# Attention and mixture-of-experts block on one core: order of the last attention group, projection in two halves, gate logits laid out by row

## The reference

```python
x = x + xattn(layernorm(x), ctx_512, Wq, w_kc_q, w_kc_kv, W_qr, W_kr, Wo)
x = x + ffn(layernorm(x), gate_weight, bias, w1, w3, w2, ws1, ws3, ws2)

# in xattn
attn    = softmax(scores)                       # per head
ctx_c   = einsum('bhsl,bld->bhsd', attn, kv_r)  # the value products
ctx_lat = einsum('bhsd,hkd->bhsk', ctx_c, w_kc_kv)
return ctx @ Wo.T                               # the projection

# in ffn
logits = x @ gate_weight.T
scores = sigmoid(logits)                        # then the routing
topk_idx, tw = choose 2 of 4 groups, then 4 of 32 experts by scores + bias
return sum over chosen experts of tw * swiglu_e(x) + swiglu_shared(x)
```

## Time and profile before

| | |
|---|---|
| median of three runs | 302.06 us |
| profiled execution, its own time | 301.82 us |
| span of the profiled execution | 299.5 us |
| outside the span | 2.3 us |
| PE busy | 282.5 us, 94% of the span |
| DVE busy | 181.4 us, 61% |
| ACT busy | 156.4 us, 52% |
| share of PE in the chain that ended last | 85% |
| mean granted PE clock | 0.995 |

### The profile page before, as it was taken

One profiled execution on the slowest core, in us unless ns is written; L12 is line 12 of the kernel. 1 busy time (PEld: TensorE's weight loads), 2 busy tenths in 40 slices (PEclk: granted clock), 3 DMA queues, 4 the chain that ended last, 5 costly groups with the idle time before them and its releaser, 6 DMA issues.

```text
span 299.5 us, 5458 instructions
## 1 busy us (share of the span) xinstructions
PE 282.5 (94%) x1831; PEld 202.7 (68%) x1831; DVE 181.4 (61%) x434; ACT 156.4 (52%) x373; POOL 129.5 (43%) x121
## 2 busy tenths in 40 slices
PE   8988799999999999999999999978789999999982
PEld 6857568676777666787667777754567666676662
DVE  4877776576757777765854466158842233344676
ACT  2747469675785866777773355185212333343330
POOL 0656328791036770079940000000176555565572
PEclk9999999999999999999999999999999999999998
DMA  7962500001700001600039992402033544432234
GB/s 235 402 253 79 204 1 2 0 2 25 255 3 1 0 3 46 218 0 1 2 127 380 402 352 78 173 2 70 1 106 106 150 150 144 154 109 72 70 82 130
DMA packets 15994, 34.41 MB, mean 115 GB/s; under 512 B 2528, under 2 KB 8416, under 8 KB 15968
## 3 DMA queue, kind: packets, MB, share of 16 engines
q1 hardware_dynamic: 13664, 27.77, 26.0%
q0 software_dynamic: 2304, 6.29, 7.4%
HBM read 30.38 MB, written 3.67 MB: 114 GB/s over the span
## 4 chain that ended last, share of the span: by engine, by line
PE 85%; DVE 7%; DMA 2%; issue 2%; ACT 2%; POOL 1%; POOLq 0%; DVEq 0%; ACTq 0%
PE bank L719 10%; PE bank L612 10%; PE bank L595 9%; PE bank L583 5%; PE bank L562 5%; PE bank L584 4%; PE bank L740 4%; PE bank L456 4%; PE bank L458 4%; PE bank L457 4%; PE bank L505 3%; PE bank L708 3%; PE bank L537 3%; PE bank L685 3%; PE bank L540 3%; PE bank L463 2%
## 5 line engine op out<-in xcount | busy, mean ns | idle before, releaser
L1413 POOL DMA_INDIRECT rope<-xn_rows,idx x32 | 31.2, 974 | 83.3 <-DVE idx L1307 61.9
L893 ACT ACTIVATE prob<-bank,nmax 128x512 f32<-128x512 f32 x48 | 32.7, 685 | 38.9 <-DVE nmax L1097 38.9
L361 POOL TENSOR_TENSOR rtmp<-abuf,rope 128x512 f32<-128x512 f32 x20 | 25.7, 1284 | 60.4 <-PE bank L458 41.0
L1097 DVE TENSOR_REDUCE nmax<-bank 128x1 f32<-128x512 f32 x64 | 41.2, 685 | 8.7 <-PE bank L584 8.4
L719 PE MATMUL bank<-wall,nmat 128*64 (+1 forms) x256 | 31.2, 386 | 0.8 <-ACT nmat L968 0.8
L612 PE MATMUL bank<-pT,kvr 128*64 128x256 f32 x256 | 31.2, 386 | 0.0
L1115 DVE COPY pT<-bank 128x512 f32<-128x512 f32 x32 | 22.0, 687 | 13.1 <-PE bank L595 12.9
L583 PE MATMUL bank<-kdup,qsp 128*128 128x512 f32 x64 | 28.3, 442 | 1.2 <-ACT prob L893 1.2
L364 POOL TENSOR_TENSOR roped<-rtmp 128x512 f32<-128x512 f32 x20 | 25.9, 1295 | 1.6
L1314 DVE TENSOR_TENSOR kv<-bank,kv 128x256 f32<-128x256 f32 x16 | 6.8, 425 | 32.5 <-ACT kv L981 32.4
L595 PE MATMUL bank<-ident,prob 128*128 128x128 f32 x192 | 26.3, 273 | 0.0
(11 more groups left out here) (217 smaller groups left out, 559.8 us busy)
## 6 DMA issues: line engine op xcount, KB each, us to landing
wall<-in_w_exp SPq DMA_DIRECT2D x32, 384.0 KB, 7.5
wring<-in_w_attn SPq DMA_DIRECT2D x16, 224.0 KB, 4.3
wring<-in_w_attn SPq DMA_DIRECT2D x4, 640.0 KB, 8.1
y_rows<-nmat SPq DMA_DIRECT2D x10, 256.0 KB, 2.1
wring<-in_w_attn SPq DMA_DIRECT2D x4, 512.0 KB, 7.0
rope<-in_rope_q SPq DMA_DIRECT2D x1, 768.0 KB, 7.0
x_sb<-in_x SPq DMA_DIRECT2D x1, 512.0 KB, 3.6
xn_rows<-xn SPq DMA_DIRECT2D x4, 128.0 KB, 1.7
```

What stands on the lines that cost most here:

```text
L361: eng.tensor_tensor(t0.rearrange("p (b s) -> p b s", b=B), own.rearrange("p (b s) -> p b s", b=B), cos, ALU.mult)
L893: act.activation(probs[t % 4], s_ps[t % 3][:, :], ACT.Exp, bias=nmax[:, t:t + 1], accum_out=psum_e[:, t:t + 1]).then_inc(s_exp, 1)
L1097: dve.tensor_reduce(nmax[:, t:t + 1], s_ps[t % 3][:, :], AX.X, ALU.max, negate=True).then_inc(s_max, 1)
L1413: pool.indirect_dma_start(xg[:, u % XG, :], None, xn_dram, bass.IndirectOffsetOnAxis(idx[:, u:u + 1], 0)) \
```

## The change

Three things are changed. First, PE runs step `O 6` between `quotients(15)` and `attend(15)`; before, it came ahead of `attend(15)` with the quotients behind that. `attend(15)` now waits for ACT's copy of the quotients. Second, step `O 7` is cut in two: the half for batch 0 comes before the sums of the gate weights and waits for one `ctx` less, the half for batch 1 behind them. Third, the gate logits have the rows as PE's weights and stream the gate weights; they come out with the tokens on the partitions, in bank 6, and DVE's copy and PE's transpose fall away.

```diff
-            {0: "-P0 -P1 -P2", 2: "O0 O1 O2 O3", 8: "O4", 11: "S0", 15: "O5 O6"},
+            {0: "-P0 -P1 -P2", 2: "O0 O1 O2 O3", 8: "O4", 11: "S0", 15: "O5"},
...
             for n in range((TILES - 2 - ALAG) // 4 + 1, GRPS):
-                if n > (TILES - 1 - ALAG) // 4:
-                    attend(n)
+                pe.wait_ge(c_sum, n)
                 quotients(n)
-
+                step(NG, "O", NP - 2)
+                pe.wait_ge(c_half, n + 1)
+                attend(n)
+
+            def last_rows(k):
+
+                i = NP - 1
+                pe.wait_ge(wk_out, out_count(len(USED) - 1))
+                pe.wait_ge(c_sum, 2 * i + 1 + k)
+                for tt in range(2 * k, 2 * k + 2):
+                    mm = pe.matmul(o_ps[k][:, (tt % 2) * D:(tt % 2 + 1) * D], ctT[:, i, tt * P:(tt + 1) * P], nmat[:, i, :],
+                                   start=False, stop=(tt % 2 == 1), skip_group_check=True)
+                mm.then_inc(o_mm, 1)
+
+            last_rows(0)
             pe.wait_ge(d_gate, 48)
             pe.wait_ge(d_moe, 16)
             for dc in range(ND):
                 mm = pe.matmul(gsum_ps, ones_e[:, 0:1].to_broadcast([P, P]), gateT[:, dc, :], start=(dc == 0), stop=(dc == ND - 1))
             mm.then_inc(gs_mm, 1)
-            step(NG, "O", NP - 1)
+            last_rows(1)
...
-            def logits_T(k):
-
-                for dc in range(ND):
-                    for tt in range(2 * k, 2 * k + 2):
-                        mm = pe.matmul(lgT_ps[tt * E:(tt + 1) * E, :], gateT[:, dc, :], xraw_T[:, dc, tt * P:(tt + 1) * P],
+            def logits(k):
+
+                for tt in range(2 * k, 2 * k + 2):
+                    for dc in range(ND):
+                        mm = pe.matmul(g_ps[:, tt * E:(tt + 1) * E], xraw_T[:, dc, tt * P:(tt + 1) * P], gateT[:, dc, :],
                                        start=(dc == 0), stop=(dc == ND - 1))
-                mm.then_inc(lgT_mm, 1)
+                mm.then_inc(lg_mm, 1)
...
-                logits_T(k)
-            pe.wait_ge(lgT_ev, 1)
-            pe.transpose(g_ps, lgT, ident[:, :]).then_inc(lg_mm, 1)
+                logits(k)
             keep_busy(6)
...
-            dve.wait_ge(lgT_mm, TT // 2)
-            dve.tensor_copy(lgT, lgT_ps).then_inc(lgT_ev, 1)
-            dve.wait_ge(lg_mm, 1)
+            dve.wait_ge(lg_mm, TT // 2)
```

More of the change, by code:

```diff
@@ L160, in build @@
         o_ps = bank[0:2]
-        lgT_ps = bank[7][:, 0:P]
         g_ps = bank[6][:, 0:P]
@@ L211, in build @@
         xraw_T = pT[:, :, :, :].rearrange("p r c s -> p (r c s)")[:, 0:ND * T].rearrange("p (d t) -> p d t", d=ND)
-        lgT = masked[:, :, :].rearrange("p t e -> p (t e)")
         eq_v = prob[:, 0, :]
@@ L272, in build @@
         gs_mm = sem("gs_mm"); gate_c = sem("gate_c")
-        lgT_mm = sem("lgT_mm"); lgT_ev = sem("lgT_ev"); lg_mm = sem("lg_mm"); lg_sc = sem("lg_sc")
+        lg_mm = sem("lg_mm"); lg_sc = sem("lg_sc")
         sh1_mm = sem("sh1_mm"); sh3_mm = sem("sh3_mm"); sh_silu = sem("sh_silu"); sh_gated = sem("sh_gated")
@@ L561, in step @@
                     for tt in range(TT):
[L562 to L566, removed]
+                        pe.matmul(o_ps[tt // 2][:, (tt % 2) * D:(tt % 2 + 1) * D], ctT[:, i, tt * P:(tt + 1) * P],
+                                       nmat[:, i, :], start=(i == 0 and tt % 2 == 0), stop=False, skip_group_check=True)
                 elif kind == "S":
```

## The result

The changed kernel takes 301.00 us in the median of 17 runs (300.05 to 302.32), the kernel before 302.15 in 17 runs beside it (301.67 to 303.49). The ratio is 0.9957, 95% interval 0.9946 to 0.9968: 1.0 to 1.6 us faster. The forecast was 301.2, with a range of 300.8 to 301.75, and 0.83 us. The profiled execution took 300.88 us with a span of 298.6, where 301.0 and 298.7 were forecast.

What follows compares the result with a forecast made beforehand. PE was taken to bound the kernel (busy 94% of the span), with time to win where the chain leaves it before the sigmoid. 0.74 (projection) + 0.09 (logits) = 0.83 us off the median 302.06 gave 301.2, range 300.8 to 301.75.

Steps and rivals of the forecast that it cites:

- Where the chain leaves PE: Time comes from stretches where the chain leaves PE, with 0.71 us idle ahead of the last projection, and PE's own work.
- Quotients first: Quotients and O6 ahead of the last value products: DVE's product ends 0.53 us earlier, with no work added.
- Halves: Last projection in halves: ACT's copy of the second half at 196.50 in place of 197.24, 0.74 us earlier.
- Logits: Gate logits with rows as weights: 0.72 us of steps removed, 0.09 us added to the gain at the sigmoid.
- Both bounds named: PE's 16 weight loads 0.113 us apart and ACT's table load with its small instruction both put the sigmoid near 200.10.
- 0.16 + 0.42: In the logits, what the wider loads take back, in us, of the 0.72 us removed.
- the loads are the limit, not the rows: In the logits, the second half's rows are ready at 198.47 while PE loads the first half until 198.63.
- The gain passes to the end: All behind the sigmoid counts from it, so the gain at the sigmoid is the gain at the end.
- The size: Whole kernel: 0.74 + 0.09 = 0.83 us gained, put on the median of 302.06.
- Slower: Rival at the logits: loads overlap nothing, 0.22 us apart, sigmoid 0.77 us later, time 302.8; 5%.
- half of it is absorbed: Rival: quotients wait for DVE or gather transfers take longer, 0.3 to 0.5 us lost, gain 0.4, time 301.65; 13%.
- More than forecast: Rival at the logits: ACT's load does not bind and PE's loads run faster, 0.74 + 0.37 = 1.1 us, time 300.95; 12%.

Runs made afterwards that it cites:

- hq: The changed kernel with the old logits, so quotients ahead and projection in halves only: 301.36 us, ratio 0.9973 to the kernel before.
- after: The changed kernel with all three changes, first trace: median 301.00 us, ratio 0.9957 to the kernel before; the profiled execution took 300.88 us.
- l_only: The kernel before with only the logits laid out by row: 301.64 us, ratio 0.9984.
- l_twice: The changed kernel with each logits matmul made twice, 32 weight loads in place of 16: 302.88 us, ratio 1.0029 to the kernel before.
- hl: The changed kernel with the quotients behind the value products again, halves and logits by row kept: 300.96 us, ratio 0.9967 to the kernel before.
- g_late: The changed kernel with the gate sums behind the second projection half and DVE's centring between its statistics pairs: 300.69 us, ratio 0.9968 to the kernel before.

## Why the prediction was right

- **Where the chain leaves PE.** Right. The idle 0.71 us is gone. The starts forecast up to the copy of the second half lie within 0.08 us on the trace's own clock, most of them within 0.03; counted from the last scores they come up to 0.15 late, the copy itself 0.07.
- **Quotients first.** The times were nearly right (DVE at 194.16, forecast 194.14, or 0.10 late counted from the last scores), the account was not. I wrote that 0.53 us of the gain "comes from the product being early". The halves alone give 0.78 us with the product as late as before; the early quotients on top of them cost 0.10 with the old logits and give 0.23 with the new ones. What they buy is the first copy of the rows free of the table load.
- **Halves.** 0.74 forecast; counted from the last scores the second copy moved by 0.67, so the term was 0.07 too large. Most of that arises by the start of the value products, 0.06 late, behind the wait ahead of the quotients. Two errors behind it cancel: the first half held PE for 0.97, not 0.88, and the gate sums for 0.36, not 0.45.
- **Logits.** 0.09 forecast on top, 0.14 found (hq to after). Both bounds named were there: loads 0.111 apart, and ACT's table load. In l_only 0.72 us of steps gone gave 0.15, because the 16 loads take longer than the old matmuls, and because ACT, whose small instruction started at 200.67 in the kernel before, could not have begun the sigmoid ahead of 200.78 with the same 0.11 behind it. The sum had 0.31 for the last matmul, where its own row said 0.28, and its line "0.16 + 0.42" leaves 0.14, not the 0.09 that it adds. The step "the loads are the limit, not the rows" is confirmed by l_twice, hl and g_late.
- **The gain passes to the end.** Sigmoid to gather is 14.51 to 14.53 in all traces in which the clock did not fall in it, before and after.
- **The size.** 0.82 us in the trace against 0.83; 1.0 to 1.6 in the times. That the trace agrees to 0.01 is partly luck: one term was 0.07 too large, the other 0.05 too small. The difference of about 0.3 to the times is open. A rarer stretch at the lower clock explains less than 0.1 of it, as the clocks of the runs show; whether it falls better in the changed kernel is not shown.
- **The rivals.** None came in full. *Slower* is out, since the loads overlap. Of *half of it is absorbed* a small part came: PE took the quotients at 190.07, with DVE's reciprocals done at 189.92 and O5 by its measure elsewhere through at 189.93. The 0.14 us between is probably a wait for DVE, where the forecast had 0.03, and such a wait was one of its signs of being wrong. *More than forecast* has a slip in its sum: from the logits' result (199.22 + 0.66) to the sigmoid at 200.93 are 1.05 us, which less one scaling of 0.29 is 0.76, not 0.37.

## What to carry to other kernels

Parts of one chain do not add: take each away alone and in pairs, and read the sum from the trace, since what a part is worth depends on which of two late inputs the others leave. Before an idle gap is filled by splitting the work behind it, look at what small work stood in the gap for free; here the gate sums moved onto the path, and a gap 170 us earlier had room for them. When steps between two engines are removed, look for a fixed cost on the receiving engine, such as a table load, that ends where the removed steps ended.

## What the runs showed of the hardware

PE's records can be full while its clock falls. In l_twice PE was busy for 3.00 of 3.00 us from 197 to 200, from 197.37 on with matmuls of 128 columns of weights and 32 streamed, and the granted clock was 0.52 in the next 3 us. In the changed kernel the same work is half as long, matmuls of 512 streamed columns follow from 199.49, and the clock stayed at 1.00 from 197 to 206.
